# Dummy identity products on TensorE in ten waits of a decoder layer with routed experts

## The reference

```
x = x + self_attention(layernorm(x), w_qkv, w_out)   # 16 heads of 32, causal
x = x + cross_attention(layernorm(x), ctx, wq, wk, wv, wo)   # one head; keys and values: ctx and x itself
x = x + experts(layernorm(x), wg, W, b)   # each token: its best of 8 experts, times its softmax gate
```

## Time and profile before

| | us |
|---|---|
| median of 3 runs | 728.16 |
| the three runs | 728.03, 728.16, 732.74 |
| the profiled execution | 735.02 |
| its span, first to last instruction | 733.3 |
| mean granted TensorE clock of it | 0.971 |
| TensorE busy, matmuls | 667.4 (91%) |
| VectorE busy | 546.6 (75%) |
| GpSimd busy | 317.8 (43%) |
| ScalarE busy | 308.0 (42%) |

### The profile page before, as it was taken

One profiled execution on the slowest core, in us unless ns is written; L12 is line 12 of the kernel. 1 busy time (PEld: TensorE's weight loads), 2 busy tenths in 40 slices (PEclk: granted clock), 3 DMA queues, 4 the chain that ended last, 5 costly groups with the idle time before them and its releaser, 6 DMA issues.

```text
span 733.3 us, 18925 instructions
## 1 busy us (share of the span) xinstructions
PE 667.4 (91%) x5896; PEld 590.0 (80%) x5897; DVE 546.6 (75%) x1657; ACT 308.0 (42%) x991; POOL 317.8 (43%) x545
## 2 busy tenths in 40 slices
PE   4768999999999989898999999999999997778994
PEld 4658888889898978796989898989898986657773
DVE  4766878787888877882678787878787868676563
ACT  3445656666565756661413141414141535222220
POOL 4377657575757675761500101010101341536652
PEclk9978999999999989999999999999999999889997
DMA  7385775665565655871960607070704682856520
GB/s 257 120 180 132 123 141 126 143 123 136 124 143 114 143 115 108 178 148 46 359 216 1 166 7 167 5 170 2 165 7 144 192 161 78 286 132 194 164 87 3
DMA packets 143070, 97.26 MB, mean 133 GB/s; under 512 B 110766, under 2 KB 114990, under 8 KB 142640
## 3 DMA queue, kind: packets, MB, share of 16 engines
q1 hardware_dynamic: 137360, 84.10, 47.2%
q0 software_dynamic: 5664, 12.61, 5.8%
HBM read 58.24 MB, written 18.77 MB: 105 GB/s over the span
## 4 chain that ended last, share of the span: by engine, by line
PE 37%; DVE 5%; issue 3%; DMA 3%; POOL 2%; ACT 1%; DVEq 1%; another core or an unknown queue 0%; SPq 0%; ACTq 0%; POOLq 0%
PE b_bank L65 35%; DMA bias_sb<-in_bias 1%; DVE w_lo L1577 1%; DMA bias_sb<-in_wo 1%; PE b_bank L1479 1%; PE b_bank L1887 1%; DVE w_lo L1117 1%; POOL w_lo L1360 1%; DVE xr L1948 1%; POOL stage L1047 1%; DVE b_smax L1593 1%; ACT w_hi L1406 0%; ACT w_hi L1416 0%; DVE c_xt_lo L1958 0%
## 5 line engine op out<-in xcount | busy, mean ns | idle before, releaser
L513 ACT ACTIVATE prob<-prob,shift 128x128 f32<-128x128 f32 (+1 forms) x256 | 114.6, 449 | 118.4 <-POOL shift L424 117.9
L65 PE MATMUL b_bank<-w_hi 128*128 128x256 f32 (+1 forms) x528 | 107.4, 326 | 4.0 <-DVE w_lo L1577 3.7
L65 PE MATMUL a_job<-w_hi 128*128 128x256 f32 (+1 forms) x488 | 96.0, 320 | 15.2 <-DVE w_lo L716 7.6
L1406 ACT CAST w_hi<-b_bank 128x256 fp32r<-128x256 f32 (+1 forms) x128 | 52.8, 450 | 127.8 <-PE b_bank L65 115.7
L65 PE MATMUL b_bank<-w_hi,w_lo 128*128 128x256 f32 (+1 forms) x528 | 104.0, 319 | 0.0
L65 PE MATMUL b_bank<-w_lo,w_hi 128*128 128x256 f32 (+1 forms) x528 | 104.0, 319 | 0.0
L737 DVE CUSTOM_DVE_ANT_0 prob<-a_s,mask 128x128 f32<-128x128 f32 (+1 forms) x256 | 79.8, 348 | 32.0 <-PE a_s L613 31.9
L65 PEld LDWEIGHTS a_job<-w_hi 128*128 128x128 f32 x488 | 72.4, 198 | 25.1 <-DVE w_lo L716 7.8
L65 PEld LDWEIGHTS b_bank<-w_hi 128*128 128x128 f32 x528 | 81.2, 192 | 11.9 <-DVE w_lo L1577 5.1
L65 PE MATMUL a_job<-w_lo,w_hi 128*128 128x256 f32 (+1 forms) x488 | 88.6, 305 | 0.0
L745 DVE TENSOR_TENSOR p_part<-prob,p_part 128x384 f16<-128x384 f32 x128 | 78.9, 616 | 13.0 <-POOL p_part L431 11.6
(11 more groups left out here) (195 smaller groups left out, 1114.3 us busy)
## 6 DMA issues: line engine op xcount, KB each, us to landing
stage<-in_w SPq DMA_DIRECT2D x5, 1024.0 KB, 10.1
xin<-in_x SPq DMA_DIRECT2D x8, 512.0 KB, 4.1
xr<-in_x SPq DMA_DIRECT2D x8, 512.0 KB, 3.9
x<-xr SPq DMA_DIRECT2D x8, 512.0 KB, 3.2
xin<-x SPq DMA_DIRECT2D x8, 512.0 KB, 8.5
stage<-in_ctx_t SPq DMA_DIRECT2D x8, 512.0 KB, 3.6
stage<-in_ctx SPq DMA_DIRECT2D x8, 512.0 KB, 4.8
xr<-x SPq DMA_DIRECT2D x8, 512.0 KB
```

Of the source, the lines that this page charges most:

```text
L65: ins = pe_matmul(out, a, b, start=first and i == 0, stop=last and i == len(steps) - 1)
L513: a = nc.scalar.activation(prob[:, e % NPROB, cols], prob[:, e % NPROB, cols], ACT.Exp, scale=-1.0, bias=shift[:, e, q:q + 1], accum_out=r ...
L1406: nc.scalar.copy(hi, src).then_inc(job_hi, 1)
```

## The change

A helper issues a number of products of the 128x128 float32 identity with itself. It is called in ten places: before X0 (32 products) and q0 (14) of the prologue, in `values` of group 0 of batch 0 (10) behind the wait for the values' middle parts, in slot 12 of batch 0 before the scores (24), in the last batch of cross-attention before p0 (11), p1 (11), y0 (6) and Y0 (14), and before the transposes of block 1 (4) and the product of block 0 (7). Each writes into the bank, or the part of one, that the operation behind it overwrites with its own first pass, after the wait for that bank and before the operation's other waits. No other engine's instructions change.

```
+        BUSY = {"X0": 32, "q0": 14}
...
             def job(j, n):
                 b, i = bank(j), int(j[1])
                 toks = slice(i * P, (i + 1) * P)
                 chunks = range(DC)
+                if isinstance(n, int) and n < 0 and j in BUSY:
+                    if last_in_bank(j, n):
+                        pe.wait_ge(job_ev, job_at(*last_in_bank(j, n)) + 1)
+                    keep_busy(nc, b[:, 0:P], ident, BUSY[j])
                 if j == "X0":
                     pe.wait_ge(xn_ready, (n + 2) * TB)
...
                 wait(pe, on_done, before)
+                if isinstance(of, int) and of == 0 and g == 0:
+                    keep_busy(nc, o_ps[:, 0, 0:P], ident, 10)
                 for j in range(HG):
                     pe.wait_ge(pt_in[j], before * 16 + 16)
...
                 s = head_at(h, 0, n)
+                if isinstance(n, int) and (n, h) == (0, 12):
+
+                    pe.wait_ge(job_ev, job_at(*last_in_bank("q0", n)) + 1)
+                    keep_busy(nc, bank("q0")[:, 0:P], ident, 24)
                 if s is not None and s % HG == 0:
                     scores(s // HG, n)
...
+        BUSY = {"p0": 11, "p1": 11, "y0": 6, "Y0": 14}
...
             def job(j, n):
                 wait_bank(j, n)
                 b, i = bank(j, n), int(j[-1])
+                if order(n) is LAST and j in BUSY:
+                    keep_busy(nc, b[:, 0:P], ident, BUSY[j])
...
         def transposes(i, k):
             m = number_of(i, k)
+            if isinstance(i, int) and k == 1:
+                keep_busy(nc, t_ps[k][:, 0:P], ident, 4)
             pe.wait_ge(rows_in[k % RX], (turn(i, k) + 1) * 16)
...
+            if isinstance(i, int) and k == 0:
+                keep_busy(nc, y_ps[k][:, 0:P], ident, 7)
             pe.wait_ge(xt_done, m + 1)
```

## The result

The changed kernel takes 739.46 us (median of 4 runs, 738.06 to 741.75) against 729.61 us for the kernel before in the same session (4 runs, 728.03 to 732.74): ratio 1.0149, 95% interval 1.0116 to 1.0181. The ratio is estimated from the single executions; the quotient of the two medians is 1.0135. The kernel is slower by about 1.5%; forecast were 736.3 us, and slower with a chance of 0.54. Single profiled executions say less here than medians: the 86 later executions of the kernel before lie between 726.0 and 737.3 us though nothing in it changes. The profiled execution of before took 735.02 us, that of the changed kernel 738.06 us, so the two traces differ by 3.0 us where the medians differ by 9.9.

What follows compares the result with a forecast made beforehand. TensorE, with 37% of the span on the chain, was taken to bound the kernel. Prologue +5.0, slots +0.5 and last batch +2.6 sum to +8.1 us on the 728.16 us median: 736.3 us, range 724 to 745.

Steps and rivals of the forecast that it cites:

- The price of a product: All ten places: each identity product costs TensorE 0.23 us at full clock and 0.43 us at the low clock.
- Rival (1): All places: products are cheap, 0.11 us each, giving about 723 us, or 718 without the tail's low stretches; chance 0.13.
- rival (4): All places: products do not hold the clock, no gain anywhere, every product 0.43 us, 754 us; chance 0.05.
- Prologue: X0's 32 and q0's 14 products: q0's four jobs end 5.0 us later, bounds +2.9 and +8.7.
- VectorE's split meets GpSimd: Prologue, upper bound: GpSimd's two-input operation blocks the split between X0 and X1, wait ends at 17.6 instead of 15.3.
- between, as the gap here is shorter: Prologue: q0's 14 uncovered products taken at 4.6 us, between 3.2 at full clock and 6.0 at low clock.
- Slots: Slots 10 and 12 of batch 0, 10 and 24 products: net +0.5 us, bounds -1.6 and +3.3.
- Given back: 62.5 to 65.9 at full clock, of which I take 1.2: Slots term: that low stretch runs at full clock, giving up to 1.7 us, 1.2 taken since VectorE paces part.
- Last batch: Places from p0 to block 0's product: +2.6 us at VectorE's finish of block 0, bounds +1 and +4.
- If the load takes as long as now: Last batch: condition for +2.6 us at block 0's finish, which starts when the later-issued bias load has come.
- Rival (2): Whole kernel: the waits absorb the products, clock held before q0, no blocking, +2 to +3, 731 us; chance 0.17.
- Rival (3): Prologue: clock falls between X0 and q0, GpSimd blocks VectorE, 14 products at low clock, 743 us; chance 0.12.

Runs made afterwards that it cites:

- e1: Only the 32 products before X0, none in the other nine places, against the kernel before: 733.92 us, ratio 1.0049.
- e11: The change without q0's 14 products, all else as changed, against the kernel before: 739.4 us, ratio 1.0104.
- e10: Only X0's 32 products, with GpSimd's value weights made to wait for VectorE's weight splits, against the kernel before: 734.45 us, ratio 1.0039.
- e9: The change with all ten counts at zero, only its two added waits left, against the kernel before: 731.24 us, ratio 1.0007.
- e3: Only the products in slots 10 and 12 of batch 0 (10 and 24), against the kernel before: 733.33 us, ratio 1.0033.
- e4: Only the six places of the last batch and first two blocks (11, 11, 6, 14, 4, 7), against the kernel before: 733.48 us, ratio 1.0032.
- e2: Only the 14 products before q0 of the prologue, against the kernel before: 736.25 us, ratio 1.0090.
- e8: The change with q0's 14 products put ahead of their wait, into k0's bank, against the kernel before: 737.68 us, ratio 1.0111.
- e7: Only the 11 and 11 products before p0 and p1, against the kernel before: 732.37 us, ratio 1.0036.
- e12: Only the 14 products before Y0, against the kernel before: 732.96 us, ratio 1.0008.
- e5: Only X0's products, 16 instead of 32, against the kernel before: 731.85 us, ratio 1.0022.
- e6: The change with counts cut to fit the waits and products issued ahead of them, against the kernel before: 733.1 us, ratio 1.0041.

## Why the prediction was right, point by point

The sign, the median and the range hold (739.5 in 724 to 745). The sum was +8.1 us on the median; measured are +9.9 between the medians, and 1.16% to 1.81% by the interval, so 8.5 to 13.2 us: the forecast lies just under it. The prologue's mechanism held and its size lies between its bounds, the term of the slots was mis-sized, and that of the last batch had the right size by a path that the traces do not show.

**The price of a product** held: 0.22 to 0.23 and 0.43 us, as forecast. Rival (1), cheap products, falls by it. So does rival (4): the clock rises under products of an identity alone, at the start and in 54.7 to 60.2.

**Prologue, forecast +5.0.** X0 was forecast at 11.8 with bounds of 11.2 and 12.2; the executions gave 10.78 to 12.22, so the bounds were too narrow on the early side. "VectorE's split meets GpSimd" was an upper bound, and it turned out a matter of the execution: in after the split kept its 0.68 us, in e1 and e11 it took 2.56 and 2.82. The wait ended at 14.15 instead of 15.3, 3.2 us behind X0's start (forecast 3.5). The step that failed in size is the 14 products: taken at 4.6 "between, as the gap here is shorter", they took 3.15 at the full clock, which the gap between X0's transposes and them did not end: 2.16 us idle, then the products. The question "which?" was a real one: 2.25 us idle in e10, with q0 behind them and no products, were followed by the low clock. Head 0's scores are 3.3 us later than in e9 and 2.6 later than in before's profile. In the times the part is larger: e1 is +3.6 us, and q0's products another 3.3 (after against e11, with the doubt said there), together 6.9, between the forecast and its upper bound of +8.7.

The parts do not add. X0, q0, slots and last batch alone make 0.49 + 0.90 + 0.33 + 0.32 = 2.04%, the change 1.49%. Part of the reason is in the timelines of the prologue: the 14 products of q0 take 4.93 us alone and 3.15 behind X0's 32, and they keep the clock that e1 loses (7.40 us for the four jobs against 5.94).

**Slots, forecast +0.5.** This is the mis-sized term: e3 measures +2.4. "4.0 late, 1.7 come through" was near (5.3 late, 2.2 come through in e3; in the changed kernel 4.3 and 1.2, each against e9 and counted from head 0). Its upper bound of 5.6 late is not worked out there; by its own prices the lateness with the first ten at the low clock is 4.3+5.5-3.3 = 6.5 us at most. What failed is "Given back: 62.5 to 65.9 at full clock, of which I take 1.2". That low stretch belonged to the one profiled execution: e9 has granted 1.00 there without any product, and of the nine profiles without products in the slots only before's has a low stretch that begins between 60 and 70 us. So in most executions there was nothing to give back. The reading had called the stretch of 267.3 chance and had not asked the same of this one.

**Last batch, forecast +2.6.** e4 measures +2.3. Counted from the rank counts in before and after: p1 +3.2 (forecast 3.4), y0 +2.2 (2.1), Y0 +3.5 (3.3), the low part of block 0 +2.75 (2.6), the issue of the bias load +2.6 (2.6). Then the profiles part from the forecast. First before's, then after's DMA issue of the load, with the time from issue to landing last; then from before's chain that ended last:

```profile
bias_sb<-in_bias SPq DMA_DIRECT2D x1, 1024.0 KB, 11.0
```

```profile
bias_sb<-in_bias SPq DMA_DIRECT2D x1, 1024.0 KB, 7.8
```

```profile
632.43 10.99 DMA bias_sb<-in_bias
```

After's chain in the same place has no load in it but TensorE's products, and then VectorE:

```profile
633.47 3.12 PE b_bank L58 x28
...
637.47 0.89 PE b_bank L58 x8
...
638.80 1.56 PE b_bank L58 x14
...
642.66 1.70 PE b_bank L1554 x16
...
647.98 0.70 DVE xr L1976
```

The low part and the finish of block 0 in after's timeline, then the finish in e1's:

```profile
638.12 0.69 DVE L1986 TENSOR_TENSOR c_xt_lo<-b_bank,c_xt_hi 128x512 fp32r<-128x512 f32 x1 [0.38 <-ACT c_xt_hi L1881]
...
647.98 0.69 DVE L1976 TENSOR_TENSOR xr<-b_bank,bias_sb 128x512 f32<-128x512 f32 x1 [0.95 <-DMA bias_sb<-in_bias]
```

```profile
644.77 0.69 DVE L1976 TENSOR_TENSOR xr<-b_bank,bias_sb 128x512 f32<-128x512 f32 x1 [0.96 <-issue]
```

The finish of block 0 comes after 0.95 us of idle time, not 3.47, and 0.3 us earlier counted from the rank counts. The row of after still names the load, but the load issued at 639.73 landed 7.8 us later, 0.45 before the finish started. And the same 0.95 or 0.96 stands ahead of it in e9, e2 and e8, and in e1, e3, e10 and e11, where the view names no releaser. So this idle time does not measure the load. Where it is longer (1.19 in e4, 1.32 in e7, 1.47 in e12, 1.71 in e5, 2.03 in e6) the load is the last to come, by 1.1 us at most. What VectorE waits for ahead of it are the logits (`L1554`), which stand behind the products of Y0 and the 4 and 7 in TensorE's order. The finish comes 38.2 to 38.5 us behind the rank counts in the four profiles with all six places, and 36.8 to 37.0 in e1, e3, e9 and e10 (35.2 in e2, 36.2 in e5): at least 1.2 us come through there.

"If the load takes as long as now" is the step that did not hold, and with it "they cost nothing as long as that load is the last to come". The load took 11.0 us in before's profile, 9.2 in e9, 7.8 in after, 7.2 in e7; of the 11.0, 2.74 are the issuing instruction, which takes 0.47 to 0.55 in the others. Before's is the only one of the fourteen profiles with this load in its chain. So the +2.6 of the forecast was reached by luck: right in size, by a path that is the chain of no other profile. It is also why the profiles of before and after hide the cost of the last batch and the medians don't. The rest of e4's 2.3 us is not placed. In e7's profile, as in e5's without these products, the chain runs here through a load of expert weights (`xn_sb<-in_w`, 12.6 and 13.3 us); that p0's and p1's lateness reaches the end by it is possible and was not followed. From the rank counts to TensorE's last matmul the profiles without products in this part take 114.1 to 117.6 us, those with all six places 116.0 to 118.8.

**The step from one profiled execution.** "728.16 plus 8.1" treated the terms as independent of that execution, and two were not (the stretch of 62.5, the load of 11.0). "Faster jobs give back 3 us" holds only where the clock stays up: the four jobs take 5.9 us in the change, e2 and e8, 6.8 in e5 and e6 (a wait between them), and 7.4 in e1, e10 and e11, against 8.6 in before. e5 and e6 show that an early start there is worth nothing, so what was booked as a gain is one only against the lateness that the products themselves cause. A late start is not swallowed by batch 1: e1 is 4.9 us late at head 0 and 5.6 at batch 1 against e9, e2 2.9 and 3.4, e10 1.6 and 2.5. That is "nothing later absorbs it" as far as a profile shows it; at the end the times of e1 and e10 are alike although their profiles are 3 us apart here.

**Rival (2)**, the waits absorb it (731), is excluded by the interval. **Rival (3)** (743) has its parts in some executions and not together. VectorE is held up in e1 and e11, and there the clock does fall again, though only after q0 has begun; neither has the 14 products. In the two profiles that have them behind X0's, after and e8, the split was not held up by more than 0.7 us and the 14 ran at the full clock. An execution of the change in which VectorE is fully blocked was not profiled; the three slower ones of the four (738.95 to 741.75) may hold it. Rival (4)'s price was too low by its own terms (34 products at 0.43 less 3.3 and 2.3 are +9 in the slots, not +5), which does not save it.

## What to carry to other kernels

Products that only hold TensorE's clock lie on TensorE's path from the moment at which the wait that they were to fill would have ended, and behind that wait they lie on it whole (q0's 14: 3.15 and 4.93 us). What of it reaches the end depends on the slack behind: 5.3 us late became 2.4 in the slots, and 14 products at Y0 cost nothing that can be measured. Here 133 of them bought some 10 us of full clock and cost 1.5%: the mean granted clock rose in every version of the whole change (after, e8, e11), and no version was faster. So a stretch at half clock is worth removing only where TensorE's late work is what others wait for; that is the reading of these runs, not a test of its own. And a gain or a cost read from one profile (a low stretch, a long load) should be asked for in a second profile first: of the three on which this forecast leaned or stumbled, two were in that one profile alone, and the third, at 267 us, in five of fourteen.

## What the runs showed of the hardware

- The same code reached the full clock 3.0 to 6.0 us after steady products began, in seven executions; with it a neighbour's collision (VectorE's split with GpSimd's) came and went, 0.68 to 2.82 us.
- With 2.2 to 4.4 us of idle time behind X0's transposes and ordinary projections after it, the clock fell again for 3.4 us in three of three executions (e1, e10, e11). With the 14 products there it did not in two of two (after, e8).
- The granted clock of the records reads 1.00 before the first change of clock though matmuls run at half rate: e2's 28 records from 11.90 take 4.93 us, after's 28 from 14.15 take 3.15. The start of a kernel has to be judged by durations.
- VectorE's operation with two inputs in SBUF was held up by a cast of GpSimd as well as by its two-input operation (e8, 1.38 us instead of 0.68), and where both started together the cast was the longer one (after, 1.59 us instead of 1.04).
- A load of 1 MB issued at the same place took 7.2 to 11.0 us from issue to landing in different executions, 2.2 us of the spread being the issuing instruction itself. VectorE's operation behind it has 0.95 us of idle time ahead of it even when the load has long landed, and the view can name the load all the same.
- With nothing changed, executions of this one-core kernel spread over 1.5% (726.0 to 737.3 us). The mean clock explains only part of it: among the 28 or 29 executions of each session the correlation of time and clock is -0.38 to -0.56.
